# Turned rows of the first stage kept in memory for the first local attention, first blocks at half width, and the closing stage's attention output in whole tiles

## The reference

```
xn = layernorm(x)                              # 4 x 1024 x 256
s  = causal_attention(xn; 16 heads of 16) @ W_o.T
y  = xn
for l in range(2):                             # two layers
    h = shift_token(y)                         # channels 128..255 from the token before
    q, k, v = split(h @ wqkv[l], 3)            # 8 heads of 64
    q, k = rotary(l2norm(q) * qs, l2norm(k) * ks)
    # blocks of 128 tokens; a block sees itself and the block before it,
    # j == -1 (before the first block) is masked
    y = y + local_attention(q, k, v) @ wo[l]
    h = layernorm(shift_token(y)) * g + b
    a, g = split(h @ w1[l] + b1[l], 2)
    y = y + (a * gelu(g)) @ w2[l] + b2[l]
out = x + s * silu(y)
```

## Time and profile before

| | |
|---|---|
| median of 3 runs | 1991.68 us (1991.46 to 1992.77) |
| the profiled execution, its own time | 1988.55 us |
| its span | 1986.7 us |
| granted PE clock, mean | 0.969 |
| PE / DVE / ACT / POOL busy | 1852.9 / 1505.5 / 1221.0 / 985.1 us |

### The profile page before, as it was taken

How to read it: one execution, slowest core, us unless ns; L and a number is a source line. 1 busy time by engine, 2 the same in 40 slices (tenths; PEclk the granted TensorE clock), 3 DMA queues, 4 the chain that set the end, 5 groups by cost and what they waited for, 6 DMA issues and landing times. The chain is left out here.

```text
span 1986.7 us, 39477 instructions
## 1 busy us (share of the span) xinstructions
PE 1852.9 (93%) x12960; PEld 1327.6 (67%) x12960; DVE 1505.5 (76%) x4145; ACT 1221.0 (61%) x2522; POOL 985.1 (50%) x807
## 2 busy tenths in 40 slices
PE   5879999999997999999997999989999999789998
PEld 4723333333333788888876788868888888667887
DVE  5778888888881899999996544379999999755543
ACT  3516666666665678777775434267788877544443
POOL 4532223222223777777772433277777777333433
PEclk9969999999998999999998999989999999889999
DMA  6993546456420000000022121100000002222212
GB/s 206 305 194 46 66 64 84 65 69 84 60 37 22 14 27 27 27 27 27 26 69 66 64 80 53 56 11 25 27 27 27 27 27 72 59 80 75 88 51 86
DMA packets 142261, 126.31 MB, mean 64 GB/s; under 512 B 31090, under 2 KB 124718, under 8 KB 141998
## 3 DMA queue, kind: packets, MB, share of 16 engines
q1 hardware_dynamic: 140782, 123.36, 27.2%
q10 hardware_dynamic: 1344, 1.31, 0.2%
HBM read 82.41 MB, written 41.96 MB: 63 GB/s over the span
## 5 line engine op out<-in xcount | busy, mean ns | idle before, releaser
L663 ACT ACTIVATE ca_pr<-ca_pS 128x1024 f32<-128x1024 f32 (+3 forms) x384 | 296.6, 811 | 205.7 <-PE ca_pS L577 165.0
L492 POOL TENSOR_SCALAR_AFFINE_SELECT ca_pr<-ca_pr 128x256 f32<-128x256 f32 x256 | 103.8, 409 | 371.4 <-ACT ca_pr L663 367.1
L691 DVE CUSTOM_DVE_ANT_0 ca_masked<-ca_pR,ca_later 128x256 f32<-128x256 f32 (+3 forms) x512 | 235.8, 485 | 42.4 <-PE ca_pR L553 38.6
L553 PE MATMUL ca_pR<-ca_ks,ca_qs 96*128 96x512 bf16 (+3 forms) x768 | 220.7, 346 | 9.2 <-DVEq L747 5.7
L695 DVE TENSOR_REDUCE ca_mx<-ca_pR 128x1 f32<-128x512 f32 x256 | 175.5, 686 | 24.9 <-PE ca_pR L553 23.1
L577 PE MATMUL ca_pS<-ca_qs,ca_ks 98*128 98x512 bf16 (+3 forms) x768 | 184.6, 331 | 9.5 <-issue 4.2
L553 PEld LDWEIGHTS ca_pR<-ca_ks,ca_qs 96*128 96x128 bf16 x768 | 70.7, 98 | 164.9 <-DVE ca_mx L691 90.8
L982 ACT ACTIVATE w_pe<-w_sm,w_nmax 128x256 f32<-128x256 f32 x256 | 126.7, 496 | 69.2 <-DVE w_nmax L1115 69.1
L905 POOL TENSOR_TENSOR w_tsn<-w_qk,w_tab 128x512 f32<-128x512 f32 x62 | 128.3, 2090 | 79.1 <-DVE w_pn L1124 79.1
L905 POOL TENSOR_TENSOR wb_tsn<-wb_qk,wb_tab 128x512 f32<-128x512 f32 x62 | 127.4, 2075 | 80.5 <-DVE wb_pn L1124 80.5
L598 PE MATMUL ca_pO<-ca_pr,ca_va 128*32 128x512 f32 (+3 forms) x1536 | 165.2, 502 | 1.6 <-POOL ca_pr L492 1.2
(11 more groups left out here) (289 smaller groups left out, 5462.6 us busy)
## 6 DMA issues: line engine op xcount, KB each, us to landing
QKP<-p_parts SPq DMA_DIRECT2D x32, 384.0 KB, 5.2
ca_qs<-QKP SPq DMA_DIRECT2D x96, 128.0 KB, 6.6
ca_ks<-QKP SPq DMA_DIRECT2D x96, 128.0 KB, 7.1
w_xt<-X SPq DMA_DIRECT2D x64, 128.0 KB, 2.0
X<-w_x SPq DMA_DIRECT2D x64, 128.0 KB, 1.7
f_hh<-X SPq DMA_DIRECT2D x32, 256.0 KB, 6.2
p_xin<-x SPq DMA_DIRECT2D x8, 512.0 KB, 5.8
X<-p_xn SPq DMA_DIRECT2D x8, 512.0 KB, 5.0
```

Of the source, the lines that this page charges most:

```text
L553: pe.matmul(bank[:, 0:w], qs[0:SHIFT_ROW, u, h, i * P:(i + 1) * P], ks[0:SHIFT_ROW, u, h, k0:k0 + w], start=True, stop=True).then_inc(ring ...
L663: act.activation(pr[:, k % 2, pair, :, 0:w], pS[:, pair, :, 0:w], ACT.Exp, scale=CS).then_inc(p_ready, 1)
L691: dve.tensor_tensor_reduce(masked[:, jb % RING, 0:w], pR[jb % RING][:, 0:w], later[:, 512 - w:512], -1.0, BIG, ALU.add, ALU.min, mx[:, i, ...
```

## The change

1. Project's SP list also stores `thi` and `tlo` of each super-tile to a new DRAM tensor `HT` (512 KB each, 16 transfers), in columns with one blank column ahead of each sequence; two transfers of 4-byte elements write the blanks for the shifted half. ACT and DVE wait for these stores before they write the buffer again, and the stage ends when they have landed.
2. In layer 0 `turn_h`, `turned` and `lo_of` do nothing. PE's `project` waits for `turned_loaded` instead, which four transfers of 64 KB raise for each window (`load_turned`). SP issues windows 0 and 1 in the causal stage, and window w+2 in its step of window w, ahead of the wait for `x1_ready(w)`. `hs` isn't loaded in layer 0. Layer 1 keeps its turns.
3. In both layers the first block of a sequence takes 128 keys: scores, mask, exponentials, normalising, `turn_p`, the copies and `values` at half width or half number. Its mask goes, and so do two memsets ahead of each layer. For that the loops run over 8 windows in a turn, not 4.
4. In the closing stage `attend` does a whole super-tile at once, at the third of the four down products (the second in the last tile), into `pT` (the last two tiles into `pH`), and `down` no longer waits for the gate. ACT runs a Gelu of one column right after the Silu of each tile (tiles 0 to 4).

```diff
@@ phase_project, SP
+            sp.wait_ge(K.made, 7)
+            for part in range(2):
+                sp.dma_start(HT[part, 1].rearrange("p (g r) -> p g r", r=SEQ + 1)[:, :, 0:1], K.blank[:, :, :],
+                             allow_slow_non_contiguous=True).then_inc(K.zeroed, 16)
...
+            def store_turned(s, j):
+                col = s * SUP * P + s * SUP // TPB + 1
+                for part, (t, done, stored) in enumerate(((thi, t_hi, hi_stored), (tlo, t_lo, lo_stored))):
+                    sp.wait_ge(done, ONE + s + 1)
+                    sp.dma_start(HT[part, :, :, col:col + SUP * P].rearrange("k p c -> p k c"), t[:, j].bitcast(F32))\
+                      .then_inc(stored[j], 16)
             def rest_of(s, j, it):
                 for g in range(CG):
+                    if g == 2:
+                        store_turned(s, j)
...
+                act.wait_ge(hi_stored[j], ONE + s // 2 * 16)
...
+                dve.wait_ge(lo_stored[j], ONE + s // 2 * 16)
@@ phase_causal, SP
                 load_rows(sp, W, 0, X)
+                for w in range(2):
+                    load_turned(sp, W, HT, w, w, w // TPB)
                 load_qkv(sp, W, 0, wqkv)
...
+def load_turned(sp, W, HT, w, j, batch):
+    for t, part in ((W.thi, 0), (W.tlo, 1)):
+        for k in range(KD):
+            sp.dma_start(t[:, j % 2, k].bitcast(F32), HT[part, k, :, bass.ds(w * P + batch + 1 - k, P)])\
+              .then_inc(W.sems["turned_loaded"][j % 2], 16)
@@ phase_window, SP
             def step(w, j, it):
                 if isinstance(w, int) and w == NW - 4:
                     start_feed()
+                if layer == 0:
+                    nxt = ahead(w, j, it, 2)
+                    if nxt:
+                        sp.wait_ge(S["v_ready"], ONE + w + 1)
+                        load_turned(sp, W, HT, nxt[0], nxt[1], nxt[2])
                 sp.wait_ge(S["x1_ready"], ONE + 2 + g0 + w + 1)
@@ phase_window, PE
             def turn_h(w, j, it):
-                pe.wait_ge(S["x_loaded"][j], ONE + (layer * (NW // 4) + it + 1) * 32)
+                if layer == 0:
+                    return
...
             def project(w, j, it):
-                pe.wait_ge(S["t_lo"], ONE + g0 + w + 1)
+                if layer:
+                    pe.wait_ge(S["t_lo"], ONE + w + 1)
+                else:
+                    pe.wait_ge(S["turned_loaded"][j % 2], ONE + (it * 4 + j // 2 + 1) * 64)
...
-                    for s in range(2):
+                    for s in blocks(j):
@@ phase_feed, PE
+                    if closing and s >= 1 and n == (2, 1)[last(s)]:
+                        attend(s - 1)
                     if closing and s == L and n == SUP - 1:
-                        attend(s - 1, n)
-                        for i in range(SUP):
-                            attend(L, i)
-                        pe.wait_ge(O.prod_ready, ONE + L * SUP)
-                    elif closing and s >= 1:
-                        pe.wait_ge(O.prod_ready, ONE + max((s - 1) * SUP + n - 1, 0))
+                        attend(L)
@@ phase_feed, ACT
+                    if s < NS - 1:
+                        act.wait_ge(O.warm, ONE + s - 2)
+                        act.activation(O.junk[:, :], lng[:, 0:1], ACT.Gelu).then_inc(O.warm, 1)
```

More of the change, by code:

```diff
@@ L115, in phase_project @@
         xn_stored, part_stored, v_stored = K.stored
+        hi_stored, lo_stored = ([sem(f"p1_{n}_stored{i}") for i in range(2)] for n in ("hi", "lo"))
         t_ready, t_hi, t_lo = sem("p1_t_ready"), sem("p1_t_hi"), sem("p1_t_lo")
@@ L193, in _ @@
                                    base=0, pattern=[[-1, P]], channel_multiplier=1).then_inc(K.made, 1)
+            pool.memset(K.blank[:, :, :], 0.0).then_inc(K.made, 1)
             pool.sem_inc(part2, CG)
@@ L224, in window_masks @@
                 m = K.masks[:, :, :].rearrange("p m (s t) -> p m s t", s=2)
-                for kind in range(3):
-                    own = kind // 2
-                    pool.affine_select(out=m[:, kind, own], in_=m[:, kind, own], compare_op=ALU.is_ge, fill=NEG,
+                for own in range(2):
+                    pool.affine_select(out=m[:, own, own], in_=m[:, own, own], compare_op=ALU.is_ge, fill=NEG,
                                        base=0, pattern=[[-1, P]], channel_multiplier=1).then_inc(masked, 1)
[L230 to L235, removed]
+                    prev = m[:, own, 1 - own]
+                    pool.affine_select(out=prev, in_=prev, compare_op=ALU.is_ge, fill=NEG,
+                                       base=0, pattern=[[1, P]], channel_multiplier=-1).then_inc(masked, 1)
             def first():
@@ L818, in steps @@
     def steps(e, step):
[L819 to L823, removed]
+        with e.Fori(0, NW // TPB - 1) as it:
+            for j in range(TPB):
+                step(it * TPB + j, j, it)
+        for j in range(TPB):
+            step(NW - TPB + j, j, NW // TPB - 1)
     def ahead(w, j, it, n):
@@ L1206, in step @@
                 if a1:
-                    maxima(w + 1, (t + 1) % TPB, 0)
+                    maxima(*a1, 0)
                 if a3:
@@ L1210, in step @@
                 if a1:
-                    maxima(w + 1, (t + 1) % TPB, 1)
+                    maxima(*a1, 1)
                 residual(w, j, it)
@@ L1218, in _ @@
             for w in range(NW):
-                step(w, w % 4, w // 4, w % TPB)
+                step(w, w % TPB, w // TPB)
         @block.tensor
@@ L1241, in project @@
                         pe.wait_ge(S["v_copied"], ONE + g0 + w)
[L1242 to L1243 removed]
+                        if layer and isinstance(w, int) and w == 0:
+                            pe.wait_ge(S["t_lo"], ONE + 2)
                     cols = slice(z * INNER, (z + 1) * INNER)
@@ L1265, in values @@
                     pe.wait_ge(S["pt_last"], ONE + g0 + w + 1)
-                for s in range(2):
-                    vj = j if s == j % 2 else (j - 1) % 4
+                for s in blocks(j):
+                    vj = (j if s == j % 2 else j - 1) % 4
                     for hh in range(2):
@@ L1343, in score @@
                         bank, slot = score_place(2 * c + r)
-                        ins = pe.matmul(pS[:, bank, slot], qt[rows, c, :], kt[rows, c].rearrange("p s t -> p (s t)"),
-                                        start=True, stop=True)
+                        keys = len(blocks(j)) * P
+                        ins = pe.matmul(pS[:, bank, slot, 0:keys], qt[rows, c, :],
+                                        kt[rows, c].rearrange("p s t -> p (s t)")[:, 0:keys], start=True, stop=True)
                 ins.then_inc(S["s_ready"], 1)
@@ L1837, in down @@
                     ins.then_inc(S["o_ready"], 1)
-                    if closing and s == 1 and n == 0:
-                        pe.wait_ge(O.wo_split, ONE + 2)
-                    if closing and s >= 1 and (s < L or n < SUP - 1):
-                        attend(s - 1, n)
             pe.wait_ge(S["w_split"], ONE + 4 * layer + 1)
```

162 lines of the change are left out of this document (89 added, 73 removed).

## The result

The changed kernel takes 2227.93 us (median of 4 runs, 2226.49 to 2228.59), where the kernel before takes 1991.57 us on the same chip: ratio 1.118, 95% interval 1.117 to 1.120. It is slower by 236 us; 2216 was forecast. The profiled execution took 2226.49 us with a span of 2224.8. The spans differ by 238.1 us.

| stretch | before | after | difference | forecast |
|---|---|---|---|---|
| start of the program to causal | 113.1 | 130.7 | +17.7 | +18 |
| start of causal | 34.0 | 37.0 | +3.0 | +2 |
| rest of causal | 483.2 | 481.5 | -1.8 | 0 |
| local attention, layer 0 | 438.4 | 668.1 | +229.6 | +229 |
| feed, layer 0 | 216.4 | 219.0 | +2.6 | 0 |

The account below looks back on a forecast made before the run. PE, without idle time in local attention's 12.83 us windows, was taken as the bound. +230 + 9 + 18 + 2 - 1 - 20 - 14 = +224 on 1988.55 gave 2212.6; with 3.1 for the median, 2216 us, range about 2150 to 2275.

Parts of the forecast that it names:

- The loads, the term that decides: Layer 0's windows 1 to 29: PE waits 6.3 us each for turned rows queued behind the previous tile's `x1_ready`; bounds 5.5, 7.0.
- `start_feed`: Step of window 28: the load for window 30 stands behind 14 DMAs in SP's list, +9 us once.
- The clock: Layer 0: each pause brings half clock behind it, costing 2.0 us a window, range 0 to 3.2.
- Rival 2: Layer 0: the pause costs no clock, so 58 us come off, giving 2158 us; chance 12%.
- Row turns: Layer 0's windows: PE no longer turns the rows, saving 0.35 us a window.
- Project: Project's super-tiles each store 1.05 MB more with DMA engines nearly full: +18 us, bounds 8 to 25.
- First blocks: Eight first windows of sequences at half width save PE 2.5 us each: -20 us, bounds -10 and -23.
- Closing stage: Closing stage: PE's waits for gate products and behind table loads, 16.1 us, mostly go: -14 us, bounds -6 and -16.
- the windows' term: Layer 0: wait 6.3 plus clock 2.0 less row turns 0.35, +7.95 us a window, 29 of them +230.

Follow-up runs that it names:

- the early loads: The changed kernel with the four loads of turned rows asked for one step earlier in SP's list: 1997.76 us, ratio 1.003 to the kernel before.
- the loads ahead of the store: The changed kernel with the four loads issued right behind the wait for `x1_ready`, ahead of the tile's store and the row load: 2189.82 us.
- the fastest kernel: The changed kernel without turned rows from Project, windows written out, POOL's addition ahead of the inverse norm: 1966.67 us, ratio 0.987 to the kernel before.

## Why the prediction was right, and where it was not

**The loads, the term that decides.** Right in mechanism and size. The pause is 6.01 us where I took 6.3; the early loads remove it entirely, the loads ahead of the store shorten it by 1.24, both by nothing but SP's order. `start_feed` cost 11.7 us and not 9: the pause there is 10.8 longer, as the loads behind it also landed 1.5 us later (3.3 us from the end of the last issue to PE's product, where it is 1.8 at 1039.73), and the step begins with 5.6 us at half clock in place of some 4.

**The clock.** Right: 20.37 less 12.44 of work less 6.01 is 1.9 us, half of the 118 us that PE works at half clock is 2.0 in each of 29 windows, and I took 2.0. Filling the pause gave 1.57 back in each window and 42 us in all; the products did not reach quite as far as the pause. (What the prediction calls the cost of the pauses of the earlier trace rows, 3.3 us or more, is how long the clock was down; half of that is the cost.) Rival 2 (2158) would have needed the fall to lie within the pause; it begins there, at 1036.55, but PE resumes before it ends.

**Row turns.** Full size, 0.39 us, only when POOL's loop is shorter; with the early loads, 0.1 us. In the changed kernel the pause left POOL time, and the full size fits: 20.37 less 6.01 less the 2.0 counted at half clock is 12.4 us of work.

**Project.** +17.7 against +18, and +15.7 by the stores alone. The size is right; that it fits to 0.3 us is luck. In the traces the causal stage starts at 111.7 to 115.8 us without the stores and at 126.4 to 132.3 with them. The ceiling of 435 GB/s from the Trainium skill's page "DMA: Bandwidth & Descriptors", section "Where 436 GB/s comes from", by which the term would have been 0, is not reached: 331 GB/s with all DMA engines busy. The prediction passed over a line of that section, which puts the limit for transfers between HBM and SBUF at about 358 GB/s; by that, an estimate from that page of the Trainium skill, the 4.4 MB of a super-tile take 12.3 us and the term is 9, half of what came.

**First blocks, the step that failed.** "I take 2.5 each, -20", with bounds of -10 and -23, came out as about nothing. "DVE ... loses a similar share ..., so it doesn't take over" looked at busy shares, and not at the loop through POOL, and the loop's length was not costed at all. Three things took the gain. The jump over eight windows costs PE 1.3 to 1.7 us by itself, and 2.1 to 3.1 beside narrow windows, mostly with half clock behind it; why the pause is longer there was not tried. That is four times, and writing the windows out gave 9 to 12 us. Behind a first window, POOL, DVE and POOL form a loop of 12.9 us, since DVE's scaling is held up by POOL's addition; with that moved a first window is worth 12.77 x 3 - (11.92 + 12.13 + 12.77) = 1.5 us, without it 0.6. And PE itself can't give 2.84. Its timeline in such a step of the fastest kernel:

```profile
1616.92 0.60 PE L1275 MATMUL wb_pX<-ident,wb_pn 128*128 128x128 f32 x4
1617.77 0.71 PE L1275 MATMUL wb_pX<-ident,wb_pn 128*128 128x128 f32 x4 [0.25 <-ACT wb_v L1023]
1618.32 0.66 PE L1329 MATMUL wb_pX<-ident,wb_qkn 128*128 128x128 f32 x4
...
1619.34 1.09 PE L1288 MATMUL wb_pX<-wb_pt,wb_v 128*64 128x128 f32 x16
1621.14 0.30 PE L1244 MATMUL wb_pX<-ident,w_xt 128*128 128x128 f32 x1 [0.71 <-issue]
```

The turns take 1.4 us and not half of the 1.85 in the earlier trace rows, as PE waits for a copy of ACT between them. From the first value product to the row turns it is 1.80 against 1.90, with 0.71 idle. The scores alone shrink nearly as reckoned, by some 0.8 where half of 1.93 was taken.

**Closing stage.** -13.6 against -14, but this match is partly luck. `base`'s wait of 8.8 us is gone. The other two waits of the earlier trace rows, 7.3 us together, gave 0.4: the warming Gelu is worth nothing, since a DVE subtraction of 3.0 us covers the table load. What filled up the sum nobody had reckoned with: PE is busy for 232.6 us in the stage where it was 236.0, for the same 1384 products, of which only the order and the PSUM banks changed. Why they take less was not looked into.

The profiled executions are 238 us apart where the sum was 224. Of the 14 us some 10 are the first blocks of layer 1 and 3 the feed of layer 0. That stage took 216.8 us in the traces with the filled pause and with the loads first, which have the same feed, so the 3 are not clear of the scatter. In layer 0 the same miss of 10 was hidden, and that is luck again: the windows' term was 230 and came out as 29 x 7.56 = 219 (the pause 0.3 shorter than taken, the clock 0.1 and the turns 0.04 better), with `start_feed` 2.7 more.

The range has a slip. The text on the clock gives 0 and 3.2 us as its bounds, the range uses 1.0 and 2.8; and with 274, 25 and the small gains (-10, -6) its upper end is 2285 and not 2275. The measured time lies inside either way.

## What to carry to other kernels

Ask of each load not how long it takes, but what stands ahead of it in its queue and whether any of that waits for the engine that needs the load: if so, no buffer depth helps, and the price is the chain plus the clock that the pause costs. When work of the limiting engine is halved in one place, write down the loop through the other engines at that place, with what holds each of them up; a busy share of 92% does not show it. A loop body made longer for static indices has a price at its jump, so compare it with the same code written out.

## What the runs showed of the hardware

- **A pause filled with useless work made the kernel faster**: 42 us for some 780 products more, the granted clock 0.98 in place of 0.83.
- **Pauses at a jump**: behind those of 1.3 us the clock stayed 1.00, behind one of 3.07 us the next 3 us were granted 0.50 (1.2 GHz). Between these the length of the pause does not tell. In layer 1 of the changed kernel the clock held behind the longer pause, of 2.54 us, and fell behind the shorter, of 2.23; the step behind the second is 1.6 us longer. In the columns of the earlier trace rows, first the one and then the other:

```profile
1665.80:1668.80 3.00, 3.00 (x13) 2.50 (x14) 2.96 (x10) 0.60 (x1) 0.64 (x1) 1.00 0.28 71
1769.10:1772.10 3.00, 3.00 (x10) 2.43 (x11) 2.96 (x10) 0.61 (x2) 0.89 (x1) 0.72 0.27 74
```

- **DVE and POOL**: four scalings of 128x256 take 1.82 us when they begin under POOL's addition of 128x1024 and 1.14 under its power of 128x16, though both read and write SBUF. The Trainium skill, page "SBUF — State Buffer", section "Who interferes with whom", has POOL and a DVE operation in a mode of two ports, which a scaling can be in, exclude each other for a whole instruction. The addition agrees (the scalings go on when it ends, at 1669.98); the power doesn't: three of the four scalings start before its end at 1665.73 and take 0.35 us each, as the one behind it does. Why these two differ was not tried.
